# Eight halves of the second layer's own products made behind the edge loop's join instead of within the loop

## What is computed

```python
def _rgcn_edge_conv(h, xe, src, dst, etype, w, rt, b):
    m = jax.nn.relu(h[src] + xe)
    seg = etype * n + dst
    mean = segment_sum(m, seg) / maximum(segment_sum(ones, seg), 1)
    out = jnp.einsum('rnd,rdo->no', mean.reshape(R, n, -1), w)
    return out + h @ rt + b

h = relu(layernorm(x))
for l in range(2):
    h = _rgcn_edge_conv(h, xe, src, dst, edge_type, weight[l], root[l], bias[l])
    h = batch_norm(h, gamma[l], beta[l])      # over all nodes
    if l == 0: h = relu(h)
return x + h
```

## Time and profile before

| | us |
|---|---|
| three executions | 2613.45, 2644.66, 2651.92 |
| their median | 2644.66 |
| the profiled execution, its own time | 2613.75 |
| its span in the profile | 2611.8 |
| second layer's edge loop, about | 1376 to 2344 |
| join, until the first turn of the chunk loop | 2344 to 2357 |
| second layer's chunk loop | 2357 to 2477 |
| last stage | 2487 to 2612 |

### The profile page before, as it was taken

How to read it: one execution, slowest core, us unless ns; L and a number is a source line. 1 busy time by engine, 2 the same in 40 slices (tenths; PEclk the granted TensorE clock), 3 DMA queues, 4 the chain that set the end, 5 groups by cost and what they waited for, 6 DMA issues and landing times. The chain is left out here.

```text
span 2611.8 us, 50770 instructions
## 1 busy us (share of the span) xinstructions
PE 2281.5 (87%) x18308; PEld 2156.6 (83%) x18308; DVE 1928.2 (74%) x5090; ACT 972.7 (37%) x2076; POOL 1541.0 (59%) x1375
## 2 busy tenths in 40 slices
PE   1299999998999999999779999998989999988966
PEld 1199998888888888899778999888988888888945
DVE  7489998888888887578766877756766677756654
ACT  0145555455455445344312222222222222224555
POOL 7656666667676666600176777777777777761000
PEclk7599999999999999999979999989999999999976
DMA  9746765656566555399833444333333334328799
GB/s 344 263 150 177 208 201 174 180 170 186 175 187 180 161 173 159 105 373 418 327 104 114 125 121 123 112 106 101 113 113 107 113 107 120 96 91 306 284 371 405
DMA packets 368342, 486.15 MB, mean 186 GB/s; under 512 B 42760, under 2 KB 274426, under 8 KB 368088
## 3 DMA queue, kind: packets, MB, share of 16 engines
q1 hardware_dynamic: 300242, 303.02, 36.1%
q0 software_dynamic: 46192, 99.84, 12.9%
q10 hardware_dynamic: 21654, 79.99, 7.6%
HBM read 306.81 MB, written 175.88 MB: 185 GB/s over the span
## 5 line engine op out<-in xcount | busy, mean ns | idle before, releaser
L1584 PE MATMUL ps_y<-arena 128*128 128x128 f32 x11032 | 1441.7, 280 | 83.2 <-issue 60.8
L1584 PEld LDWEIGHTS ps_y<-arena 128*128 128x128 f32 x11032 | 1350.4, 196 | 137.9 <-issue 115.2
L1193 DVE SCALAR_TENSOR_TENSOR arena<-arena 128x512 f32<-128x512 int32 (+1 forms) x1386 | 852.4, 684 | 296.8 <-remote 192.5
L845 POOL DMA_INDIRECT acc<-arena x550 | 601.6, 1094 | 261.6 <-issue 147.7
L830 POOL DMA_INDIRECT arena<-h_rows,arena x394 | 482.9, 1226 | 346.2 <-DMA h_rows<-chunk_mem 185.6
L830 POOL DMA_INDIRECT arena<-in_x_dram,arena x394 | 439.3, 1115 | 210.2 <-issue 108.0
L1388 ACT ACTIVATE arena<-ps_y 128x512 f32<-128x512 f32 (+1 forms) x198 | 117.9, 595 | 854.6 <-remote 479.7
L1585 PE MATMUL ps_y<-arena 128*128 128x128 f32 x1576 | 315.0, 281 | 7.9 <-issue 7.3
L1596 PE MATMUL ps_o<-arena 128*128 128x128 f32 x1576 | 234.9, 282 | 47.7 <-issue 46.3
L1380 ACT ACTIVATE arena<-ps_t 128x512 f32<-128x512 f32 (+1 forms) x198 | 116.3, 587 | 417.6 <-remote 296.0
L1596 PEld LDWEIGHTS ps_o<-arena 128*128 128x128 f32 x1576 | 201.1, 193 | 73.0 <-issue 71.5
(11 more groups left out here) (249 smaller groups left out, 2100.2 us busy)
## 6 DMA issues: line engine op xcount, KB each, us to landing
arena<-in_edge_attr_dram SPq DMA_DIRECT2D x190, 256.0 KB
arena<-in_edge_type_dram SPq DMA_DIRECT2D x190, 256.0 KB
chunk_mem<-acc SPq DMA_DIRECT2D x55, 512.0 KB, 14.0
acc<-arena ACTq DMA_DIRECT2D x28, 896.0 KB
acc<-arena SPq DMA_DIRECT2D x28, 896.0 KB
arena<-in_x_dram SPq DMA_DIRECT2D x45, 512.0 KB, 9.8
arena<-acc SPq DMA_DIRECT2D x43, 512.0 KB, 12.1
chunk_mem<-hn_rows SPq DMA_DIRECT2D x41, 512.0 KB
```

The lines of the kernel that those rows point to most:

```text
L845: pool.indirect_dma_start(out=acc[l], out_offset=at(idx_t[:, t:t + 1]), in_=ob[:, gg % OB, t // NG, :], in_offset=None, **how).then_inc(co ...
L1193: ins = v.scalar_tensor_tensor(mk[:, m, r, 0:n], types, float(r), mt[:, gg % MT, 0:n], ALU.is_equal, ALU.mult)
L1584: te.matmul(ps_y[gg % 2][:, c], mk[:, gg % MKS[l], r, c], w_sb[l][:, r * D:(r + 1) * D], start=r == 0, stop=False)
```

## The change

The halves 36 to 43 (the chunks 32, 34, 36 and 37 of `OWN_FIRST`) are taken out of the edge loop and made one after the other directly behind the join's matmuls, by the same four functions. The first transposes of the chunk loop wait until all 44 halves are out of the bank. SP's load of a chunk's rows no longer waits for an earlier chunk's transposes, since the last of these would now come behind the loop; it waits for the landing of the load before it on the same semaphore.

```diff
     def own_half(g):
         k = (g - 6) // 2
-        return k if g >= 6 and g % 2 == 0 and k < 2 * len(OWN_FIRST) else None
+        return k if g >= 6 and g % 2 == 0 and k < LAST_HALVES[0] else None
+    LAST_HALVES = range(2 * len(OWN_FIRST) - 8, 2 * len(OWN_FIRST))
...
                         else:
-                            sp.wait_ge(ownT_ps, 2 * (i - 1))
+                            wait(sp, own_in[i % 2], 16 * (i // 2))
                         table_dma(sp, own_at(i).rearrange("p (c d) -> p c d", d=D), h1_tab, OWN_FIRST[i], own_in[i % 2], True)
...
                 a_.activation(join_sum[:, :], ps_y[0][0:J, 0:D], ACT.Copy).then_inc(join_ready, 1)
+                if l == 1:
+                    for k in LAST_HALVES:
+                        first_turned(k)
+                        first_out(k)
...
                 last.then_inc(join_ps, 1)
+                if l == 1:
+                    for k in LAST_HALVES:
+                        first_rows(k)
+                        first_product(k)
...
                             product_added(c - 2)
+                        if c == ROWS[1][0]:
+                            pe.wait_ge(first_ready, 2 * len(OWN_FIRST))
                         if c in ROWS[1]:
                             rows_turned(c)
```

## The result

The changed kernel takes 2651.83 us (median of 22 runs, 2627.88 to 2680.99), the kernel before on the same chip 2635.32 us (22 runs, 2613.06 to 2659.37). The ratio is 1.0078 [1.0053, 1.0103], so +20.6 us (+14.0 to +27.1): slower, and within 2%. Medians here are of all executions, while ratios leave out those that are more than 1.5% above the fastest of their kernel, which is why the ratio gives 20.6 us where the medians are 16.5 apart. The profiled execution of the changed kernel took 2662.2 us.

What follows compares the result with a forecast made beforehand. Behind the join PE was taken as the bound; in the edge loop, PE with POOL leaving 0.44 us a group. -7.0 + 20.6 = +13.6 us gave 2627.4 us profiled, 2658.3 us on the median's scale, range 2614 to 2672.

Steps and rivals of the forecast that it cites:

- The chain, +20.6: Behind the join: eight serial halves take 33.3 us against a 12.73 us gap, so PE starts 20.6 us later.
- the bound of 4.60 for half clock: Behind the join: one serial half takes 4.60 us if PE runs at half clock throughout.
- the mixed clock of 0.63: Behind the join: PE's granted clock taken from the last stage's bursts, giving 4.24 us a half.
- The rival on the clock: Behind the join: the clock stays up, the chain takes 25.1 us, the whole is +2.6 us; chance 0.2.
- The loop, -7.0: Edge loop: without the eight halves, POOL's idle time allows 0.44 us a group over 16 groups, 7.0 us saved.
- the bound of 10.3: Edge loop: 10.3 us would come back if PE alone set the pitch.
- POOL alone sets the loop: Edge loop: taking the halves out gives 0, so the kernel is 20.6 us slower; chance 0.2.
- The faster rival: Edge loop: PE's load stretches the pitch, which falls to 8.64 us; 26.2 us back, 5.6 us faster overall; chance 0.15.
- Caught up by the loads, 0: Chunk loop: SP's head start on loads of sums counted as 0, with 5.8 us kept as possible gain.
- the clock at the chunk loop's start, 0: First 24 transposes of the chunk loop: no change counted from the clock, with 2.8 us kept as possible gain.
- the 8.6 kept as bounds: Chunk loop: possible gains counted as 0, 5.8 us from loads caught up and 2.8 us from the clock.
- The waits ahead of `rows_turned(2)` and on SP, 0: Chunk loop's new wait for a copy and SP's changed wait for an earlier load: both cost nothing.

Runs made afterwards that it cites:

- warm: The changed kernel with idle transposes of the identity on PE, six ahead of each product behind the join and four behind it: 2654.36 us, 1.0044 of the kernel before.
- banks_again: Second measurement of the changed kernel with its eight halves behind the join overlapped over four PSUM banks instead of one: 2636.14 us, 1.0009 of the kernel before.
- again: The changed kernel unaltered, measured a second time: 2704.34 us, 1.0032 of the kernel before.
- drop: The changed kernel with the last eight halves left out altogether: 2694.04 us, 0.9971 of the kernel before.
- banks: First measurement of the changed kernel with its eight halves behind the join overlapped over four PSUM banks instead of one: 2692.85 us, 0.9958 of the kernel before.
- banks_third: Third measurement of the changed kernel with its eight halves behind the join overlapped over four PSUM banks instead of one: 2604.46 us, 1.0004 of the kernel before.
- chain_only: The kernel before with its loop untouched and eight more halves made serially behind the join: 2725.72 us, 1.0108 of the kernel before.
- breaks: The kernel before with a one-element memset between DVE's seven masked copies in the second layer's groups: 2712.98 us, 1.0074 of the kernel before.
- four: The changed kernel with only the last four halves behind the join instead of eight: 2707.77 us, 1.0010 of the kernel before.
- pool_less: The kernel before with one of POOL's three scatters left out of each second-layer group from the 26th on: 2588.28 us, 0.9511 of the kernel before.
- gather_less: The kernel before with one of POOL's four gathers left out of each second-layer group from the 26th on: 2518.85 us, 0.9575 of the kernel before.

## Why the prediction was right, and where not

**Sign and size.** Forecast was +13.6 us on the profile's scale. Measured are +20.6 [14.0, 27.1] in the first comparison and +17 +- 6 in both. The sign, its reason (a serial chain longer than the gap) and the class within 2% held. That 2658.3 us lies so near to 2651.8 owes something to chance: the median of before turned out 9.3 us lower than the three runs shown gave (2635.3, not 2644.7), and the difference of the medians 2.9 us larger (16.5).

**The chain, +20.6: the right step, its clock mis-sized.** Measured +23.7 and +22.6. The eight halves took 37.4 us, not 33.3. A half was 4.81 us, not 4.24: 1.09 + 0.04 + 0.78 + 0.05 + 2.07 + 0.04 + 0.60 + 0.14. Even the bound of 4.60 for half clock was low, by the product's 0.15 us and ACT's 0.05. The failed step is the one that took the mixed clock of 0.63 from the last stage, "nearest to this row" by PE's busy share. The busy share was near enough (26.75 of 40 us, 67%, against 68%), the granted clock was not: 0.53. Two stretches with the same busy share may be granted different clocks; the bounds, one for each level, were the better half of that step.

**The rival on the clock.** The chain did not keep the clock up. The Trainium skill's "the default state is throttled, and activity releases the throttle" ("TensorE: Matmul & The Clock Gate", section "What's actually happening") agrees with warm and banks_again, where PE was busy 24.12 of 28 and 13.93 of 14 us and was granted 0.95 and 0.79; the chain's own 26.75 of 40 us did not release it. What this rival had right is the difference: with warm, the clock made at least 9.9 us.

**The loop, -7.0: too large, and its reason fell.** Total less P, against before, for each run (us):

| run | by the ratio | behind the join | left for the loop |
|---|---|---|---|
| changed | +20.6 +- 6.6 | +23.7 | -3.1 |
| again | +8.6 +- 10.4 | +22.6 | -14.0 |
| drop | -7.8 +- 9.7 | -1.2 | -6.6 |
| banks | -11.3 +- 9.9 | -0.3 | -11.0 |
| banks_again | +2.4 +- 9.2 | -1.8 | +4.2 |
| banks_third | +1.0 +- 5.0 | -1.1 | +2.1 |
| warm | +11.6 +- 12.9 | +12.4 | -0.8 |

Weighted by their intervals: -2.3 +- 3.0 us for eight halves; the interval is rather too narrow, since again, drop and banks share one series of the kernel before, as do banks_again and warm. The same sum for chain_only, whose loop is that of before, leaves +29.2 - 21.4 = +7.8 +- 11.1 where 0 is due, which shows how rough a single row is. For banks_third the part behind the join is the mean of the other two of its kind, since in its own profile PE waited 13.4 us for the loads of sums; by its own P of 270.8 the sum would be -3.9. So the halves bring something between nothing and 7 us when they leave the loop; the bound of 10.3 is unlikely, and -7.0 lies at the edge. The forecast's argument for it, that POOL's idle time allows 0.44 us a group, does not stand against breaks: with 44 us of POOL's time free in 200, the pitch didn't fall.

**POOL alone sets the loop.** The times can't tell this rival's 0 from the -2.3. The forecast's own sign for it, a pitch of 10.3 us, is nearer to the 10.54 than its 9.8 was: over the groups 77 to 93 the profile of before has 10.21, and none of the seven without the last eight halves in the loop lies below that (10.58 to 12.56; four and chain_only, which keep some or all of these halves there, have 10.21 and 11.35, so the spread between executions is as large as what is looked for). As a mechanism it was half right: one DMA of POOL fewer in a group brings more than 100 us (pool_less, gather_less), shorter DMAs bring nothing (breaks), and where a DMA stands in each group POOL's time alone is the pitch.

**The faster rival.** It needed a pitch below 8.99 us. The changed kernel's was 10.54 and again's 10.70. Even with one gather fewer in a group it is 9.1. What the rival had right is where PE's load lets the pitch fall to: six groups of the changed profile came every 8.5 us, where it had 8.64. But over the 16 groups it did not hold. Out.

**Caught up by the loads, 0, and the clock at the chunk loop's start, 0.** The waits for DMA fell from 5.8 to 3.2 us, and the first 24 transposes run at full clock sooner (1.04 for eight, L1657 at 2408.26, where the earlier trace rows had 1.91). The rest behind the first sums is 0.9 us shorter, 2.1 in again. In drop and four, where nothing was gained that way, it is 0.9 shorter and 1.6 longer. The shortest rest, 2.9 less, is that of chain_only. So some 1 to 3 us at most, no more than the profiles differ by in any case, of the 8.6 kept as bounds.

**The waits ahead of `rows_turned(2)` and on SP, 0.** Neither shows among the waits of the changed profile.

**The range** of 2614 to 2672 held. It was wide by the spread of the runs as well as by the causes: the causes alone gave -5.6 to +23.5.

## What to carry to other kernels

Work moved into another engine's idle gap is worth what it takes in its new form, not what it took where it overlapped: here 1.29 us of PE's time a half became 4.81 in a serial chain through one bank, and 1.30 again with four banks. Before filling a gap, write down the period of the chain at the lower clock as well, and compare both with the gap. And before taking work out of a loop, show by an experiment that the loop is bound by what it is taken from.

## What the runs showed of the chip beyond this

**A DMA of POOL stands behind DVE's copies, now and then or in every group.** In the changed kernel's second loop, from 1376 on, 182 of POOL's indirect DMAs began while DVE was within a run of its seven masked copies and at least 0.3 us ahead of its end. 165 of them took 1.53 us at most; 17 lasted until the run's end, 3.9 to 5.5 us. Fifteen of those began 0.22 to 0.23 or 0.77 to 0.78 us into the run; six that began there too did not stand. With a 60 ns memset between the copies (breaks) none of 269 did. The Trainium skill, "SBUF — State Buffer", section "Who interferes with whom", says that a DVE instruction with two SBUF inputs contends with a GpSimd instruction that reads SBUF. Of DVE's 2-port modes it says that whoever issues first has the shared ports for the whole instruction and the other blocks; and it infers that what builds a GpSimd DMA's descriptors is not held up by `tensor_tensor`, which takes the shared read side alone. The 17 agree with the first in kind, though they waited for up to seven instructions and not for one, and not with the inference; the 165 show that it is not so each time. That the shared ports are what these DMAs wait for, no run shows.

**Single stands did not matter for the time, rows of them did.** Taking away the few of an ordinary execution brought nothing (breaks). In step, one in each group, they gave 12.3 us a group in the changed kernel's profile and 12.5 in that of banks_third. The mean over the groups 77 to 93, 10.58 us, hides that, since the six groups ahead had come every 8.5. What starts such a row, and how often executions have one, no run shows.

**A serial chain on PE and ACT had the lower clock from end to end.** Behind the join the granted clock was 0.50 for 38 us in chain_only (PE busy 26.23 of 38) and in again (25.62 of 38), 0.53 in the changed kernel, and 0.95 where the same chain had its waits filled. The busy share alone does not tell the clock: the last stage of before had 0.63 at 27.29 of 40 us.
